# A differential-attention and ternary-FFN layer: the first FFN product in even blocks, two-part fp16 scores, a one-input coefficient

## The reference

```python
q = hidden_states @ Wq.T; k = hidden_states @ Wk.T; v = hidden_states @ Wv.T
# 32 query heads and 16 key heads of 16, 8 value heads of 32; rope on q and k
scores = jnp.einsum('bhqd,bhkd->bhqk', q, k) + causal
probs = jax.nn.softmax(scores, axis=-1).reshape(bsz, H, 2, tgt_len, tgt_len)
diff = probs[:, :, 0] - lambda_full * probs[:, :, 1]
attn = jnp.einsum('bhqk,bhkd->bhqd', diff, v)          # then RMS norm per head, Wo
...
h = jax.nn.gelu(jnp.einsum('bsd,fd->bsf', x, w1_q) + b1, approximate=False)
out = jnp.einsum('bsf,df->bsd', h, w2_q) + b2           # w1_q, w2_q in {-1, 0, 1}
...
x = x + _L0_attn_ref(_layernorm(x), ...)
x = x + _L0_ffn_ref(_layernorm(x), ...)
```

## Time and profile before

| what | value |
|---|---|
| median of 3 runs | 4437.56 us (4431.58 to 4438.31) |
| the profiled execution: span, first to last instruction | 4427.3 us |
| busy, share of the span | PE 81%, PEld 48%, DVE 78%, ACT 66%, POOL 33% |
| busy, us | PE 3604.6, DVE 3467.0, ACT 2909.6, POOL 1450.2 |
| mean granted TensorE clock | 0.903 |
| first row maximum of batch 0; of batch 1 | 87.4; 598.0 us |
| a batch in the loop | 533 to 536 us |
| POOL, L458 / L460 / L462, mean of one | 666 / 763 / 1164 ns |

### The profile page before, as it was taken

The page is one execution under the profiler, slowest core; times in us unless marked ns, Lnnn a source line. Parts: engine busy times, 40 slices in busy tenths (PEclk is TensorE's granted clock), DMA queues, the critical chain, the costliest instruction groups (busy, mean ns, idle before and its releaser), DMA issues.

```text
span 4427.3 us, 80970 instructions
## 1 busy us (share of the span) xinstructions
PE 3604.6 (81%) x23454; PEld 2143.3 (48%) x23454; DVE 3467.0 (78%) x6124; ACT 2909.6 (66%) x6786; POOL 1450.2 (33%) x1563
## 2 busy tenths in 40 slices
PE   2688888888788887888878988888878888888886
PEld 1345544455444554544544544455544555444553
DVE  6778877888678886788867887678877788678891
ACT  1567756677566775667756766567666677567772
POOL 0233233332333333323343323433133332333323
PEclk7789989999899899998899988999989899899898
DMA  4212112211122112112122120222112121222110
GB/s 131 51 24 43 24 43 43 38 24 30 38 43 43 22 34 48 37 32 38 25 43 43 30 37 20 44 41 43 24 41 43 24 40 24 43 43 41 21 37 14
DMA packets 146768, 166.71 MB, mean 38 GB/s; under 512 B 16640, under 2 KB 117632, under 8 KB 145792
## 3 DMA queue, kind: packets, MB, share of 16 engines
q1 hardware_dynamic: 146304, 161.13, 18.0%
HBM read 105.95 MB, written 55.12 MB: 36 GB/s over the span
## 4 chain that ended last, share of the span: by engine, by line
PE 35%; DVE 28%; issue 22%; ACT 8%; DMA 3%; SPq 2%; POOL 2%; DVEq 1%; ACTq 0%; POOLq 0%
DVE NM L665 10%; PE M L867 6%; PE M L817 6%; PE F L889 5%; PE SP_ L832 5%; PE DP L844 5%; DVE E L689 4%; DVE CC L686 3%; PE F L902 3%; ACT E L541 2%; DMA KST<-scratch 2%; PE M L811 2%; ACT L541 2%; DVE RS L684 1%; DVE NM L673 1%
## 5 line engine op out<-in xcount | busy, mean ns | idle before, releaser
L541 ACT ACTIVATE E<-SP_,NM 128x256 f32<-128x256 f32 (+7 forms) x2048 | 1518.6, 743 | 733.6 <-DVE NM L665 526.4
L665 DVE TENSOR_REDUCE NM<-SP_ 128x1 f32<-128x896 f32 (+3 forms) x1024 | 1032.6, 1017 | 225.1 <-PE SP_ L833 222.9
L832 PE MATMUL SP_<-KST,QST 96*128 96x512 bf16 (+3 forms) x3072 | 864.1, 355 | 407.7 <-ACT E L541 345.5
L689 DVE SCALAR_TENSOR_TENSOR E<-E,CC 128x512 f32<-128x512 f32 (+7 forms) x1024 | 994.6, 971 | 36.1
L553 ACT ACTIVATE DT<-DP 128x512 f32<-128x512 f32 (+3 forms) x1024 | 527.8, 515 | 546.2 <-PE DP L844 524.0
L844 PE MATMUL DP<-ident,E 128*128 128x128 f32 x3328 | 614.5, 302 | 208.6 <-DVE E L689 207.3
L673 DVE TENSOR_REDUCE NM<-SP_ 128x2 f32<-128x1024 f32 (+3 forms) x512 | 419.8, 820 | 297.2 <-PE SP_ L833 290.3
L832 PEld LDWEIGHTS SP_<-KST,QST 96*128 96x128 bf16 x3072 | 278.7, 103 | 762.7 <-ACT E L541 537.1
L844 PEld LDWEIGHTS DP<-ident,E 128*128 128x128 f32 x3328 | 391.1, 153 | 382.2 <-issue 203.1
L889 PE MATMUL F<-X2H,W1Q 128*128 128x256 f16 x2048 | 502.0, 283 | 69.9 <-ACT HP L596 65.8
L817 PE MATMUL M<-WQKV,WT 128*128 128x512 f32 x1040 | 530.8, 607 | 8.4 <-DVE T L648 4.1
(11 more groups left out here) (86 smaller groups left out, 4780.3 us busy)
## 6 DMA issues: line engine op xcount, KB each, us to landing
QST<-scratch SPq DMA_DIRECT2D x390, 128.0 KB, 4.4
scratch<-SPL SPq DMA_DIRECT2D x65, 576.0 KB, 2.8
KST<-scratch SPq DMA_DIRECT2D x390, 64.0 KB, 5.0
...
```

Of the source, the lines that this page charges most:

```text
L541: act.activation(dst, score_out(i, 2 * n + k, w), ACT.Exp, bias=NM[:, (2 * u + k) % 8:(2 * u + k) % 8 + 1], scale=1.0, accum_out=SUM[:, i ...
L665: nc.vector.tensor_reduce(NM[:, m:m + 1], score_out(i, 2 * n + k, P * (i + 1)), AX.X, ALU.max, negate=True).then_inc(max_ready, 1)
L689: nc.vector.scalar_tensor_tensor(out=E1[:, u % 2, 0:w], in0=E2[:, e:e + w], scalar=CC[:, u % 2:u % 2 + 1], in1=E1[:, u % 2, 0:w], op0=ALU. ...
L832: pe.matmul(SP_[:, k[a // 512], 0:n], q, KST[0:ROWS, a // P:(a + n) // P, kk, :], start=True, stop=not last)
```

## The change

- **Products.** `w1` is set in even blocks (from 4 on, and tail blocks 0 and 2), `w2` in odd blocks (from 5 on, and tail blocks 1 and 3); the tail has four blocks. X2H and X2L have two buffers. All half slots stay as they are.
- **Scores.** Two fp16 parts and three products: high x high, (high/64) x (64 rest), (64 rest) x (high/64), 48 rows for each of two groups of heads, on the same 96 rows. Q's other 48 rows are zero (written once, by a POOL memset), so KST holds two key heads in one column block and is half as large. POOL writes 64 x rest and high/64, two one-input instructions, in place of a copy and a subtraction with a wait between them. The stack still has six QST and six KST DMAs, each with half the bytes.
- **E2** has two units of 1024 in all blocks.
- **Coefficient.** `diff` takes the reciprocal of the second sum alone; CC is a tensor_scalar of that reciprocal with the first sum and -lambda as per-partition scalars. The first sums' reciprocals are taken once in a block, 128x16, at hs 5.
- **Gelu parts.** No factor 1/16: L460 is gone, and the output sum adds two tensors.
- **Setup.** w1 arrives in four DMAs, in KST, HH and HL; the sums of magnitudes are four reduces.

```diff
         self.finish = runs(1, (0,))
-        self.w1 = t % 2 == 1 and runs(3, (1,))
-        self.w2 = t % 2 == 0 and runs(4, (0, 2))
+        self.w1 = t % 2 == 0 and runs(4, (0, 2))
+        self.w2 = t % 2 == 1 and runs(5, (1, 3))
...
-    for t in range(3):
+    for t in range(4):
         run(QBlock(B, t, "last"))
...
-        KST = sb("KST", [P, TILES, NK, P], BF16)
-        QST = sb("QST", [P, 2, NQ, P], BF16)
+        KST = sb("KST", [P, TILES, NK // 2, P], F16)
+        QST = sb("QST", [P, 2, NQ, P], F16)
...
-        E2 = sb("E2", [P, S], F32)
+        E2 = sb("E2", [P, 2, S], F32)
...
-                for j in range(PROD):
-                    sp.dma_start(QST[DH * j:DH * (j + 1), tile % 2, :, :].rearrange("p (s c) n -> p s c n", s=8),
-                                 src[QPART[j], :, :, 0:4, :]).then_inc(stacked, 16)
+                for a in range(2):
+                    for j in range(PROD):
+                        r = PART * a + DH * j
+                        sp.dma_start(QST[r:r + DH, tile % 2, :, :].rearrange("p (s c) n -> p s c n", s=8)[:, :, 2 * a:2 * a + 2, :],
+                                     src[QPART[j], :, :, 2 * a:2 * a + 2, :]).then_inc(stacked, 16)
...
-                pool.tensor_scalar(SPL[:, 1, c], T2[:, c], 1.0, 0.0, ALU.mult, ALU.add).then_inc(mid_part, 1)
-                after(pool, mid_part, 2 * nb + part + 1)
-                pool.tensor_tensor(SPL[:, 2, c], T2[:, c], SPL[:, 1, c], ALU.subtract).then_inc(split_done, 1)
+                pool.tensor_scalar(SPL[:, 1, c], T2[:, c], LOW, 0.0, ALU.mult, ALU.add)
+                pool.tensor_scalar(SPL[:, 2, c], SPL[:, 0, c], 1.0 / LOW, 0.0, ALU.mult, ALU.add).then_inc(split_done, 1)
...
-                pool.tensor_scalar(HH[:, fs, :], HP[:, h, :], HS, 0.0, ALU.mult, ALU.add).then_inc(h_chain, 1)
-                hold(pool, h_chain, 2 * n + 1)
-                pool.tensor_scalar(HP[:, h, :], HP[:, h, :], HS, 0.0, ALU.mult, ALU.add).then_inc(h_chain, 1)
-                after(pool, h_chain, 2 * n + 2)
+                pool.tensor_scalar(HH[:, fs, :], HP[:, h, :], 1.0, 0.0, ALU.mult, ALU.add).then_inc(h_chain, 1)
+                after(pool, h_chain, n + 1)
                 pool.tensor_tensor(HL[:, fs, :], HP[:, h, :], HH[:, fs, :], ALU.subtract).then_inc(h_ready, 1)
...
-                    after(act, d_ready, b * N_U + u - (1 if i < 4 and u > 0 else 0))
-                    e = 512 * (u % 2) if i < 4 else 0
-                    dst = E2[:, e:e + w]
+                    after(act, d_ready, b * N_U + u - 1)
+                    dst = E2[:, u % 2, 0:w]
...
-                nc.vector.reciprocal(RS[:, i % 2, :, col], SUM[:, i % 2, :, col]).then_inc(d_chain, 1)
+                nc.vector.reciprocal(R2[:, u % 2:u % 2 + 1], SUM[:, i % 2, 1, col:col + 1]).then_inc(d_chain, 1)
                 after(dve, d_chain, 2 * gu + 1)
-                nc.vector.scalar_tensor_tensor(out=CC[:, u % 2:u % 2 + 1], in0=SUM[:, i % 2, 0, col:col + 1], scalar=neglam[:, 0:1],
-                                               in1=RS[:, i % 2, 1, col:col + 1], op0=ALU.mult, op1=ALU.mult).then_inc(d_chain, 1)
+                nc.vector.tensor_scalar(CC[:, u % 2:u % 2 + 1], R2[:, u % 2:u % 2 + 1], SUM[:, i % 2, 0, col:col + 1],
+                                        neglam[:, 0:1], ALU.mult, ALU.mult).then_inc(d_chain, 1)
...
+                        if hs == SUM_INVERSE:
+                            nc.vector.reciprocal(RS[:, :], SUM[:, (t - 1) % 2, 0, :]).then_inc(inv_ready, 1)
```

More of the change, by code:

```diff
@@ L58 @@
 XS = 2048.0
-HS = 1.0 / 16
-PROD = 6
-QPART = (0, 0, 0, 1, 1, 2)
-KPART = (0, 1, 2, 0, 1, 0)
-ROWS = PROD * DH
+PROD = 3
+QPART = (0, 2, 1)
+KPART = (0, 1, 2)
+PART = PROD * DH
+ROWS = 2 * PART
+LOW = 64.0
 GELU_F = FT // 2
@@ L217, in diff_attention_ffn @@
         SUM = sb("SUM", [P, 2, 2, H], F32)
[L218 removed]
+        R2 = sb("R2", [P, 2], F32)
+        RS = sb("RS", [P, H], F32)
         CC = sb("CC", [P, 2], F32)
@@ L329, in diff_attention_ffn @@
         wsum = E1[:, 1, 0:2 * 64].rearrange("p (a b) -> p a b", b=64)
-        w1f = KST[:, :, :, :].rearrange("p a b c -> p (a b c)").bitcast(F32)
-        w2f = DT[:, :, :, :].rearrange("p a b c -> p (a b c)")
+        kraw = KST[:, :, :, :].rearrange("p a b c -> p (a b c)").bitcast(F32)
+        w1f = [kraw[:, 0:FF], kraw[:, FF:2 * FF], HH[:, :, :].rearrange("p a b -> p (a b)").bitcast(F32),
+               HL[:, :, :].rearrange("p a b -> p (a b)").bitcast(F32)]
+        draw = DT[:, :, :, :].rearrange("p a b c -> p (a b c)")
+        w2f = [draw[:, FF * k:FF * (k + 1)] for k in range(4)]
         cutt = HP[:, :, :].rearrange("p a b -> p (a b)")
@@ L373, in stack @@
             def stack(nb, tile, q_free, k_free):
-                hold(sp, stacked, 16 * 2 * PROD * (nb - 1))
+                hold(sp, stacked, 64 * PROD * (nb - 1))
                 hold(sp, split_done, 2 * nb + 2)
@@ L380, in stack @@
                 hold(sp, s_ready, q_free)
-                for j in range(PROD):
-                    sp.dma_start(QST[DH * j:DH * (j + 1), tile % 2, :, :].rearrange("p (s c) n -> p s c n", s=8),
-                                 src[QPART[j], :, :, 0:4, :]).then_inc(stacked, 16)
+                for a in range(2):
[3 more added lines that the diff above has]
+                                     src[QPART[j], :, :, 2 * a:2 * a + 2, :]).then_inc(stacked, 16)
                 if k_free is not None:
                     hold(sp, s_ready, k_free)
-                for j in range(PROD):
-                    sp.dma_start(KST[DH * j:DH * (j + 1), tile, :, :].rearrange("p (s c) n -> p s c n", s=8),
-                                 src[KPART[j], :, :, 4:6, :]).then_inc(stacked, 16)
+                for a in range(2):
+                    for j in range(PROD):
+                        r = PART * a + DH * j
+                        sp.dma_start(KST[r:r + DH, tile, :, :], src[KPART[j], :, :, 4 + a, :]).then_inc(stacked, 16)
             def result(T, j):
-                k = T.t - 4 + j
+                k = T.t - 5 + j
                 hold(sp, o_ready, T.no + j + 1)
@@ L425, in _ @@
             pool.memset(onesf, 1.0).then_inc(pool_const, 1)
+            pool.memset(QST[:, :, :, :], 0.0).then_inc(q_zeros, 1)
             pool.memset(nhalf[:, :], -0.5).then_inc(pool_const, 1)
@@ L737, in dve_work @@
                             after(dve, m_wo, nf + 1)
+                            after(dve, o_sum, nf - 3)
                             nc.vector.tensor_tensor(x1, M[:, :], X[:, (t - 1) % 4, :], ALU.add).then_inc(x1_ready, 1)
@@ L773, in _ @@
             for j, (w, q, arrived) in enumerate(((w1f, W1Q, w1_in), (w2f, W2Q, w2_in))):
-                dve.wait_ge(arrived, 16)
-                link(nc.vector.tensor_reduce(wsum[:, j, :], w.rearrange("p (a c) -> p a c", a=64), AX.X, ALU.add,
-                                             apply_absolute_value=True))
+                dve.wait_ge(arrived, 64 - 48 * j)
+                for k in range(4):
+                    link(nc.vector.tensor_reduce(wsum[:, j, 16 * k:16 * k + 16], w[k].rearrange("p (a c) -> p a c", a=16), AX.X, ALU.add,
+                                                 apply_absolute_value=True))
                 nc.vector.tensor_reduce(wtot[:, j:j + 1], wsum[:, j, :], AX.X, ALU.add).then_inc(abs_sum, 1)
@@ L876, in scores_ahead, with first_product @@
                         scores(T.b, T.t, 2 * s + 1)
-            def first_product(q, k, j):
+            def first_product(T, k, j):
+                q, z = T.pair, T.t // 2 % 2
                 f = 2 * k + j
@@ L965, in pe_work @@
                     if piece and piece[1] < 2:
-                        first_product(T.pair, *piece)
+                        first_product(T, *piece)
                     if T.second_product(hs):
```

50 lines of the change are left out of this document (25 added, 25 removed).

## The result

| | before | changed |
|---|---|---|
| median | 4437.94 us | 4404.11 us |
| single runs | 4431.58 to 4443.72 | 4396.56 to 4408.19 |
| span of the profiled execution | 4427.3 us | 4406.4 us |

The ratio is 0.9923, with a 95% interval of 0.9909 to 0.9937: 34 us of gain (28 to 40) where I had forecast 84. "Faster" was right and the time lies inside the wide range (4300 to 4415), but it is 51 us above 4353 and outside the likeliest case's own range (4315 to 4395).

What follows compares the result with a forecast made beforehand. No engine owns the kernel: its chain alternates between PE and DVE, DVE nearly full in wide blocks. Terms -3-46-17-15-4+1 = -84 from span 4427.3 give 4343.3, plus 10.3: 4353 us forecast; 8-in-10 range 4300 to 4415.

Steps and rivals of the forecast that it cites:

- the wide range: Whole kernel: the 8-in-10 range of 4300 to 4415 us, leaving out the slower case and most of the 4277 one.
- likeliest case: Whole kernel: 4353 us, with its own range of 4315 to 4395; chance 0.57.
- Placement: Product 1 to even blocks, product 2 to odd: -21 body, -12 first batch, +30 tail, in all -3 us.
- The tail: End of the kernel: two product 1 and two product 2 there after the change, uncovered, +30 us.
- the first batch: Block 3 of the first batch drops its product 1: -12 us.
- The third rival: FFN blocks: odd blocks are long for another cause than product 1; slower, 4543 or 4498 us; chance 0.09.
- Coefficient: L686 on DVE becomes a tensor_scalar saving 115 ns per unit, 118 us of DVE, -46 us on the path.
- 0.42: Share of L686's time on the chain, 133 of 317.9 us, used to scale the coefficient and POOL savings.
- the second rival: DVE is the bound of all wide blocks, so each ns counts: 4277 us; chance 0.12.
- POOL less: POOL loses 234 of 1450 us, so DVE's waits for it on L686 and L689 shrink 16%: -17 us.
- Shared rows, second row: Half-size stack transfers cut PE's wait at block 1's start, -15 us; second exponential row twice, -4 us.

Runs made afterwards that it cites:

- second profile: The changed kernel unaltered, timed again as base for three follow-ups: 0.9913 of the kernel before, span 4396.1 us.
- the kernel with the products back: The changed kernel with product 1 back in odd and product 2 in even blocks, the rest as changed: 0.9771 of the kernel before, median 4334.91 us.
- gelu left out: Gelu replaced by a two-element ACT copy, in the changed kernel (0.9583 of before) and with FFN products in their old blocks (0.9496).
- copy for gelu: Gelu replaced by an ACT copy of the same 128x2048, in the changed kernel (0.9639 of before) and with FFN products in their old blocks (0.9545).

## Why the prediction was wrong, term by term

**Placement: -3 forecast, +63 measured. This is the step that failed.** The tail (+30, measured 32.8) and the first batch (-12, measured -7.4) were right in kind. The body was not: I had read from the block lengths of one batch that odd blocks would give back 26.1 and even blocks pay 23.1. The mean blocks of batches 1 to 6 of the changed kernel (second profile) against the kernel with the products back, and the same difference for the two pairs without gelu:

| us | 0 | 1 | 2 | 3 | 4 | 5 | 6 | 7 |
|---|---|---|---|---|---|---|---|---|
| forecast | +3.7 | -3.7 | +5.5 | -8 | +6.7 | -6.7 | +7.2 | -7.7 |
| measured, gelu | +6.5 | -5.4 | +10.1 | -7.4 | +7.1 | -5.2 | +4.5 | -4.0 |
| measured, gelu left out | +5.0 | -2.4 | +5.1 | -5.6 | +0.9 | -0.6 | +1.0 | +0.5 |
| measured, copy for gelu | +5.4 | -3.1 | +5.4 | -5.9 | +0.1 | +0.2 | +0.9 | -0.9 |

Even blocks pay 28.2 and odd ones give back 22.0. Two errors of mine add up. I interpolated product 1's price from the neighbours of one batch and got one that rises with the width; from block 2 on it falls. The wide blocks carry it at 4 to 7 us and, without table loads, at 1 us or less (both pairs); the narrow ones, where I had seen that "nothing is full", have less time to hide it in. Each even block is narrower than the odd one that had product 1 before. And I credited block 7 with 7.7, against 4.0: at its end PE now waits longer for the keys (26.0 us in all for 17.7 with the products back), so part of what block 7 gave back only became waiting.

Of the body's price (36.6 + 5.3 = 42 us) the copy for gelu leaves 6 x 2.0 + 3.0 = 15, and gelu left out, which takes away loads and instruction, 6 x 4.0 + 2.8 = 27. The second should not be the larger, so I take from the two only that 15 to 27 of the 42 us go with the table loads: each pair of 2.57 us costs 2.0 us in even blocks and 1.5 in odd ones (16.4 and 12.3 us a batch over eight pairs). PE's busy lines say what these are. For the same 23454 matmuls PE is busy 33.3 us longer in the changed kernel than with the products back (3624.8 for 3591.5, mean granted clock 0.900 for 0.908), and under the copy 8.3 us longer (3575.0 for 3566.7, 0.915 in both). The difference of the spans falls by 23.4 us (66.3 to 42.9), that of the busy times by 25.0: as far as the modelled ends tell, what goes with the loads is matmuls run at the lower clock rather than more waiting. What makes the rest of the 42 stays open; that narrow blocks hide less is what the table suggests, not what a run isolated.

The third rival comes nearest: even blocks pay more than odd ones give back. Its first half held (28.2, where it had 30.7). Its second, that odd blocks are long for another cause and give back a quarter or half of 26.1, did not: they gave back 22.0. So its price per batch was too high (24 or 17.6 lost, measured 6.1), and it was set to decide at 9. With 6.1 the rest of the sum won, so the sign stayed.

**Coefficient: -46 forecast, -38.6 measured, by two errors that cancel.** Its saving was sized at 115 ns per unit from VE's 155 ns; VE's form has no scalar from SBUF and the new one has two, so undisturbed it is 54 ns slower than the old. What it wins is the waits: in 1024 instances none leaves 272 to 276 ns, where the old form's mean was 297 to 310; and L696 behind it fell from 955.5 to 929.8 us. DVE's busy time fell by 45 us in all, not by 118. The other error was 0.42, the share that the chain gave this line. A line's share in one chain says where the chain happened to pass; DVE's work counted with 0.66 to 1.26 in three comparisons. This is the second rival's claim ("each ns counts"), which I had given 0.12.

The new form does not wait for POOL: its longest instance is 276 ns. That tensor_scalar can contend for the shared ports, on conditions on its operands (the Trainium skill, SBUF — State Buffer, Who interferes with whom), does not show at one element a row. At 128x512 it may: TOK's median is 541 ns and its longest 1464.

**POOL less: -17 forecast, 0 in the body of the changed kernel.** With the new form the scaling can be added again, and DVE's products wait as long as without it. I had made a wait proportional to the busy time of the engine that it names. With the old form, which does wait for POOL, some of the term may be real: L696 took 960.5 us without the scaling and 977.9 with it, but the ratios don't confirm it.

**Shared rows, second row: -19 forecast, 35.5 by the runs, 20.5 by the spans.** Right in place (KST's wait before block 1 went from 20.0 to 4.6) and too small: a third to a half of it is the first batch, where I had counted nothing. The second row's part is too small to be told apart. On the halved transfers: QST's 1024 B pieces became 512 B and the median landing fell from 4.4 to 2.4 us; KST's became 256 B and its landing fell from 5.0 to 1.9. At a change of batch less is won: at the six changes inside the loop the last of six landings takes 2.5 to 3.4 us in the changed kernel and 3.5 to 4.0 in before. The Trainium skill (DMA: Bandwidth & Descriptors, Specifications) wants 512 B or more per transfer for full rate, and I had put the term at -8 if KST gained nothing. It did gain; as bytes and pieces were halved together, no run here shows what the size of the pieces alone costs. The start of a batch gave little for another reason: PE's branch of 3.4 to 3.9 us stood beside this wait in the kernel before too, and at four of six changes its first score came 0.27 us after the branch.

All edits but the placement together: forecast -81, measured 101.6 (0.9771). The sum of the small terms was fair; one term that was a difference of two large numbers sank it.
